# Softmax attention on one core: the later query half's sums from ScalarE in query layout, maxima turned per group, and a list-scheduled order

## The chip, the cores and the metric

The kernel runs on one core of one Trainium2 chip. The metric is device time in microseconds (us). A core has five engines that run in parallel, each through its own instruction stream: TensorE (PE in the profile; its weight loads are PEld), VectorE (DVE), ScalarE (ACT), GpSimd (POOL) and SyncE (SP, which here only issues DMAs). They wait for each other through semaphores. TensorE writes to PSUM, which has 8 banks of 512 fp32 columns on 128 partitions.

## The reference

Six blocks follow one another on x of 2 x 1024 tokens of width 128: a routed feed-forward (8 experts), a gated linear attention, the same feed-forward again, a second routed feed-forward, a softmax attention, and that feed-forward again. The change touches the softmax attention alone:

```python
q = embedded @ Wq.T + bq          # likewise k and v; 16 heads of width 8
qk = jnp.einsum('bhqd,bhkd->bhqk', q, k) / jnp.float32(np.sqrt(s))
p = jax.nn.softmax(qk, axis=-1)
mask = jnp.triu(jnp.ones((s, s), dtype=p.dtype), k=0)
p = p * mask                      # after the softmax, not before it
z = jnp.einsum('bhqk,bhkd->bhqd', p, v)
x = embedded + z                  # then a layer norm with gamma and beta
```

The sequence that is run has 1024 tokens in each of 2 batches. The mask keeps keys k >= q. Since it is applied after the softmax, each query's denominator takes all 1024 keys, while its value sum takes only the keys from the query on. For the later query half (queries 512 to 1023) the keys 0 to 511 enter the denominator and nothing else.

## The kernel before

The 16 heads of the 2 batches form GR = 8 groups of 4 heads. For each group the kernel works over query tiles i (0 to 7, of 128 queries) and key tiles j (0 to 7, of 128 keys). In the plan (`attention_plan`, which returns one list that every engine walks) each item is a letter:

- A: the scores of one head and one query tile against all 1024 keys, in query layout (queries on partitions): two bf16 matmuls of 512 columns (line 770) into one of two slots of two PSUM banks each. VectorE then reduces the 1024 columns to the negative row maximum (line 1342). A slot is free again when the reduction is done (`wait_slot`). There are 256 A tiles.
- S and M: when one head has its four tiles of a query half, GpSimd splits the maxima into three bf16 parts (lines 1444 to 1447, four operations), TensorE turns them (line 778), ScalarE copies them out (line 970), and SyncE stores them as three further rows of that head's queries (line 505). The next score matmul thus subtracts the maximum by itself. There are 64 of these turns.
- B: the scores again, now in key layout (keys on partitions), of one head and one key tile against 512 queries, maximum subtracted: one bf16 matmul of 512 columns (line 795) into a ring of NBB = 3 banks, which the turns M share. ScalarE takes exp of it into SBUF, in a ring of NPT = 12 (line 987). The ring bank is free when that exp is done (`wait_ring`).
- V: for one step (one key tile, four heads) the fp32 matmuls of the probabilities with the values and with a column of ones (line 828) into the one PSUM bank that is left. The four heads stand in four column groups of TensorE and run side by side. A step whose key tile crosses the diagonal has up to three parts: `denominator` (sum alone), `both` (values and sum) and `masked` (values of the 128x128 block after GpSimd's triangle, line 1454). For the later query half the key tiles 0 to 3 are `denominator` alone, 512 columns wide.
- T: after two groups, sixteen transposes of the result (line 783) into the A slots, which VectorE divides out (lines 1356 and 1357). C, part of V in the plan before, is ScalarE's copy of the result bank (line 994).
- Z: pieces of the next layer norm of the first batch, on VectorE, with two changes of ScalarE's function table.

`STEPS` holds per group 8 steps for the earlier query half and 8 for the later one, so 16 steps of four B and one V. The order is written by rule: 20 A tiles come first, then A tiles are spread evenly between the B's (`want`), and they end 8 steps before the last step. Each V stands one step behind its B's. SyncE loads the operands of group G + 3 (lines 481 and 484) when group G is done.

## Time and profile before

| | us |
|---|---|
| median of 3 runs | 973.85 |
| lowest, highest | 973.75, 978.03 |
| the profiled execution, its time | 973.44 |
| its span in the profile | 971.7 |
| attention stage, first score matmul to the end of the last turn | 409.40 to 850.15 |

The page splits the span into 40 slices of about 24.3 us and gives the busy share of each engine in tenths:

```
PE   4042867504214965299999999999899999830794
DVE  5216599631521437596877777768977776062243
ACT  2021500203102643216877676766767777720462
PEclk9995899657555995658999999998999999965697
```

Slices 17 to 35 are the attention. A digit is an average: what decides is which engine the others wait for inside a step, and that is read from the timeline. The clock row is the clock granted to TensorE, 9 or more standing for full speed. Matmul lengths in the profile contain the time through the pipeline, so the cost of a matmul in a stream is read from the distance between starts.

### The profile page before, as it was taken

To read this page: it belongs to the slowest core of one execution; us is meant where nothing else is said; L and a number is where in the kernel's file an instruction comes from. 1 tells how busy PE (TensorE), PEld (TensorE's weight loads), DVE (VectorE), ACT (ScalarE), POOL (GpSimd) and SP (SyncE) were. 2 spreads that over 40 slices of the span, in tenths; PEclk is the share of its full clock that TensorE was granted. 3 is DMA by queue.
4 is the path that set the end of the run, shared out by engine and by line. 5 is a ranking of instruction groups with operands and counts; after the bars stand their busy time and mean duration, and the time that the engine had idled before them with its cause. 6 is when DMAs were issued, how large, how long until landed. Compare 5 with 4: busy or idle time off the path is not lost.

```text
span 971.7 us, 13757 instructions
## 1 busy us (share of the span) xinstructions
PE 671.2 (69%) x4446; PEld 331.9 (34%) x4446; DVE 571.0 (59%) x1035; ACT 443.7 (46%) x836; POOL 299.9 (31%) x679
## 2 busy tenths in 40 slices
PE   4042867504214965299999999999899999830794
PEld 4031322403213962113333333242233433230693
DVE  5216599631521437596877777768977776062243
ACT  2021500203102643216877676766767777720462
POOL 0606156151633440012233223230323233105242
PEclk9995899657555995658999999998999999965697
...
DMA packets 45926, 44.89 MB, mean 46 GB/s; under 512 B 5904, under 2 KB 36316, under 8 KB 45600
## 3 DMA queue, kind: packets, MB, share of 16 engines
q1 hardware_dynamic: 41168, 35.90, 15.8%
...
q10 hardware_dynamic: 144, 0.51, 0.2%
...
## 4 chain that ended last, share of the span: by engine, by line
PE 56%; DVE 16%; issue 8%; POOL 8%; DMA 7%; ACT 4%; SPq 1%; POOLq 0%; ACTq 0%; DVEq 0%
PE PS L828 14%; PE PS L795 12%; PE PS L770 11%; PE PS L628 5%; PE PS L639 4%; POOL slots_x L1389 4%; DVE ARENA L1342 3%; POOL ARENA L1403 2%; DVE ARENA L1312 2%; PE PS L535 2%; ACT ARENA L987 2%; DMA ARENA<-slots_x 2%; DVE XN L1042 2%; DVE PS L1304 1%; POOL ARENA L1414 1%
## 5 line engine op out<-in xcount | busy, mean ns | idle before, releaser
L1342 DVE TENSOR_REDUCE ARENA<-PS 128x1 f32<-128x1024 f32 x256 | 303.0, 1220 | 94.2 <-PE PS L770 93.7
L987 ACT ACTIVATE ARENA<-PS 128x512 f32<-128x512 f32 x512 | 279.6, 597 | 95.8 <-PE PS L795 89.3
L795 PE MATMUL PS<-ARENA 75*128 75x512 bf16 x512 | 175.0, 388 | 8.3 <-ACT ARENA L987 6.8
L770 PE MATMUL PS<-ARENA 72*128 72x512 bf16 x512 | 164.5, 406 | 21.1 <-DMA ARENA<-k_parts 16.6
L828 PE MATMUL PS<-ARENA 128*8 128x128 f32 (+8 forms) x1920 | 153.3, 435 | 0.7 <-ACT ARENA L987 0.7
L1454 POOL TENSOR_SCALAR_AFFINE_SELECT ARENA<-ARENA 128x128 f32<-128x128 f32 x256 | 74.6, 296 | 160.6 <-ACT ARENA L987 160.4
L580 PE MATMUL PS<-C,ARENA 128*128 128x128 f32 x78 | 17.1, 369 | 120.0 <-DMA ARENA<-slots_x 119.9
L1272 DVE TENSOR_TENSOR ARENA<-PS,ARENA 128x512 f32<-128x512 f32 x46 | 31.8, 692 | 96.1 <-PE PS L628 96.1
L553 PE MATMUL PS<-C,XN 128*128 128x128 f32 x96 | 24.5, 407 | 90.9 <-DVE XN L1042 89.9
L795 PEld LDWEIGHTS PS<-ARENA 75*128 75x128 bf16 x512 | 47.5, 98 | 105.6 <-ACT ARENA L987 56.8
L770 PEld LDWEIGHTS PS<-ARENA 72*128 72x128 bf16 x512 | 44.8, 100 | 103.9 <-issue 37.1
L894 ACT COPY ARENA<-PS 128x512 f32<-128x512 f32 (+1 forms) x20 | 11.5, 573 | 134.3 <-PE PS L580 134.3
L828 PEld LDWEIGHTS PS<-ARENA 128*32 128x32 f32 (+2 forms) x1920 | 43.7, 98 | 76.1 <-issue 38.7
L1396 POOL DMA_INDIRECT tokens_y<-ARENA x46 | 44.7, 972 | 74.8 <-DVE ARENA L1281 73.8
L1444 POOL CAST ARENA<-ARENA 128x4 bf16<-128x4 f32 x64 | 12.1, 189 | 174.2 <-DVE ARENA L1342 174.1
L580 PEld LDWEIGHTS PS<-C,ARENA 128*128 128x128 f32 x78 | 12.2, 188 | 123.3 <-issue 119.3
L628 PE MATMUL PS<-ARENA 128*128 128x128 f32 x368 | 53.6, 293 | 1.1 <-ACT ARENA L917 0.7
L639 PE MATMUL PS<-ARENA 128*128 x368 | 51.5, 284 | 1.5 <-ACT ARENA L928 1.5
L1414 POOL TENSOR_TENSOR ARENA<-ARENA 128x1024 f32<-128x1024 f32 x16 | 37.6, 2351 | 46.2 <-DVE ARENA L1312 44.0
L1389 POOL DMA_INDIRECT slots_x<-ARENA,SCATI x32 | 31.4, 983 | 63.7 <-DVE ARENA L1222 55.2
L553 PEld LDWEIGHTS PS<-C,XN 128*128 128x128 f32 x96 | 16.5, 208 | 97.9 <-DVE XN L1042 86.6
L1389 POOL DMA_INDIRECT slots_x<-XN,SCATI x32 | 31.3, 978 | 60.1 <-DVE SCATI L1242 51.0
...
## 6 DMA issues: line engine op xcount, KB each, us to landing
...
```

What stands on the lines that cost most here:

```text
L553: i = nc.tensor.transpose(PS[:, c % 2, (t % 4) * P:(t % 4 + 1) * P], XN[:, t, 0:P], ident)
L628: ins = nc.tensor.matmul(PS[:, 4 + i % 2, f * P:(f + 1) * P], W1[:, i % 2, f * P:(f + 1) * P], XST[:, i * P:(i + 1) * P], start=True, stop ...
L639: ins = nc.tensor.matmul(o, HG[:, i % 2, f * P:(f + 1) * P], WT[:, bass.ds(owner[i] * WB + F1 + f * P, P)], start=(f == 0), stop=(f == FB ...
L770: ins = nc.tensor.matmul(PS[:, slot + c, :], Q3[0:KQ, G % Q3R, g, i * P:(i + 1) * P], K3[0:KQ, G % Q3R, g, c * 512:(c + 1) * 512], start=T ...
L795: nc.tensor.matmul(PS[:, bank, 0:w], K3[0:MR + 3, G % Q3R, i, j * P:(j + 1) * P], Q3[0:MR + 3, G % Q3R, i, half * 512:half * 512 + w], sta ...
L828: ins = nc.tensor.matmul(PS[32 * g:32 * g + width, 7, lo:hi], v, probs, start=(what == "denominator" and st in (0, TB)), stop=(j == TB - 1 ...
L987: nc.scalar.activation(PT[:, n % NPT, 0:w], PS[:, 4 + ring_number[x] % NBB, 0:w], ACT.Exp).then_inc(b_exp, 1)
L1342: nc.vector.tensor_reduce(NM[:, k % 4, i:i + 1], PS[:, slot:slot + 2, :].rearrange("p b n -> p (b n)"), AX.X, ALU.max, negate=True).then_i ...
L1389: pool.indirect_dma_start(sx[k], bass.IndirectOffsetOnAxis(ap=SCATI[:, t:t + 1], axis=0), src[:, t, :], None, bounds_check=slots - 1, oob_ ...
L1396: pool.indirect_dma_start(ty, bass.IndirectOffsetOnAxis(ap=XS[:, i, P:P + 1].bitcast(U32), axis=0), EO[:, i, :], None, bounds_check=N - 1, ...
L1414: nc.gpsimd.tensor_tensor(QS[:, n % 8, :], QT[:, b * S:(b + 1) * S], ST[:, n % 2, :], ALU.mult).then_inc(qs_done, 1)
L1454: nc.gpsimd.affine_select(out=MD[:, n % NPT, :], in_=PT[:, n % NPT, diag:diag + P], compare_op=ALU.is_ge, fill=0.0, base=0, pattern=[[-1, P]],
```

## The change

**Fewer key-layout steps.** The later half's steps over key tiles 0 to 3 are gone: `STEPS` has 12 steps per group (96 in all, 128 before). The remaining four steps of the later half (key tiles 4 to 7) take only the query tiles that their values need, 256, 256, 384 and 512 columns (`columns`), and their `denominator` parts are as narrow.

**The missing sums in query layout.** ScalarE takes exp of the scores with the maximum as its bias and lets the accumulator output add up the row. For query tiles 6 and 7 (`DIRECT`, items X) it reads A's own slot, 768 and 896 columns, after VectorE's reduction; the slot stays taken until then. For tiles 4 and 5 (`AGAIN`, items D) TensorE computes the 512 columns once more into the ring. The exps themselves go to a scratch area (`SPARE`). Per group, four fp32 matmuls against the identity (item N) add these sums into the result bank ahead of the later half's first V. `DEN` and `SPARE` lie over weights of the first feed-forward, which are no longer in use.

**Maxima turned per group.** One S, M and copy now serve four heads (48 rows), 16 in all where there were 64. SyncE issues four row stores behind each, and the first B of a group's half waits for all four.

**The order.** `attention_plan` now simulates the engines with a table of costs (`WEIGHT`) and takes at each moment the item of the lowest rank that can start. It returns a list for each engine. The A tiles are planned to end 12 steps before the last one (`TAIL`), with at least 18 first.

```diff
 HQ = TB // 2
-STEPS = [(0, j) for j in range(TB)] + [(1, j) for j in range(TB)]
+MW = 4 * HQ
+DIRECT = (6, 7)
+AGAIN = (4, 5)
+STEPS = [(0, j) for j in range(TB)] + [(1, j) for j in range(HQ, TB)]
 NS = len(STEPS)
+FIRST = {0: 0, 1: TB}
+LEAD = 2
+TAIL = 12
...
+WEIGHT = {"A": 0.44, "M": 0.3, "D": 0.22, "T": 0.6, "N": 0.9, "max": 1.19, "split": 0.95, "mask": 0.29, "rows": 4.5,
+          "copy": 0.59, "turn": 0.9, "load": 8.0, "Z": 1.2}
+HOP = 0.1
...
+def columns(m):
+    half, j = STEPS[m % NS]
+    if half == 0:
+        return 4 * P, (P * j if j < HQ else None)
+    last = max(i for i in range(HQ, TB) if i <= j or i in AGAIN)
+    return P * (last - HQ + 1), P * (j - HQ)
+def v_parts(m):
+    half, j = STEPS[m % NS]
+    w, diag = columns(m)
+    if diag is None:
+        return [(0, w, "both" if half == 0 else "denominator")]
+    parts = [(diag, w, "denominator")]
+    if diag > 0:
+        parts.append((0, diag, "both"))
+    return parts + [(diag, diag + P, "masked")]
...
+    ahead = 4 * HQ + LEAD
...
+        if last_turns:
+            offer(-1, "T", slot_free(slots, NA), last_turns[0][0])
+        if at < len(tiles):
+            G = tiles[at][1] // 4
+            share = 1.0
+            if b < 4 * steps:
+                m, g = divmod(b, 4)
+                share = min(1.0, (done_by[m] + (done_by[m + 1] - done_by[m]) * g / 4) / done_by[-1 - TAIL])
+            rank = 0 if at < ahead + (len(tiles) - ahead) * share else 5
+            offer(rank, "A", slot_free(slots, NA), 0.0 if G < Q3R else finished.get(G - Q3R))
+        if to_turn:
+            offer(0.5, "M", slot_free(ring, NBB), to_turn[0][0])
+        if again:
+            offer(1.5, "D", slot_free(ring, NBB), again[0][0])
+        if b < 4 * steps and b < 4 * v + NPT:
+            m, g = divmod(b, 4)
+            G, (half, j) = m // NS, STEPS[m % NS]
+            offer(1, "B", slot_free(ring, NBB), rows.get((G, half)) if m % NS == FIRST[half] else 0.0)
+        if 4 * v + 4 <= b:
+            G, (half, j) = v // NS, STEPS[v % NS]
...
+            offer(1.2, "V", *times)
+        return out
...
+        kind = min((x for x in offers if x[0] <= now), key=lambda x: x[1])[2]
+        if kind == "A":
+            _, hh, i = item = tiles[at]
+            at += 1
+            now += WEIGHT["A"]
...
+            if i in DIRECT:
+                held[0] = None
+                later(top + HOP, 0, 0.18 + P * i / 1200, ("X", hh, i), then)
+            elif i in AGAIN:
+                again.append((top + HOP, hh, i))
+            if hh % 4 == 3 and i == tiles_of_unit(h)[-1]:
+                to_turn.append((run("pool", top + HOP, WEIGHT["split"], ("S", G, h)) + HOP, G, h))
+        elif kind == "M":
...
+        DEN = col("f0_w1").rearrange("p (r i c) -> p r i c", r=2, i=HQ)
+        SPARE = C[:, COLS["f0_w2"][0]:COLS["f0_b2"][0] + E * P].rearrange("p (r n) -> p r n", r=2)
...
-                        G, g = divmod(hh, 4)
+                        _, G, h = x
                         tiles = tiles_of_unit(h)
-                        sp.wait_ge(m_copied, maxima_number[hh, h] + 1)
-                        sp.dma_start(Q3[MR:MR + 3, G % Q3R, g, tiles[0] * P:(tiles[-1] + 1) * P],
-                                     MT[0:3 * len(tiles), hh % 4, :]).then_inc(m_rows[hh % 4], 16)
+                        sp.wait_ge(m_copied, maxima_number[G, h] + 1)
+                        for g in range(4):
+                            sp.dma_start(Q3[MR:MR + 3, G % Q3R, g, tiles[0] * P:(tiles[-1] + 1) * P],
+                                         MT[3 * HQ * g:3 * HQ * (g + 1), h, :]).then_inc(m_rows[h], 16)
...
+                    elif i in DIRECT:
+                        pe.wait_ge(x_exp, direct_number[k, i] + 1)
...
+                    elif kind == "D":
+                        G, g = divmod(k, 4)
+                        nc.tensor.matmul(PS[:, bank, :], Q3[0:KQ, G % Q3R, g, i * P:(i + 1) * P],
+                                         K3[0:KQ, G % Q3R, g, 0:512], start=True, stop=True).then_inc(d_scores, 1)
+                    elif kind == "N":
+                        pe.wait_ge(x_exp, 4 * len(DIRECT) * (k + 1))
+                        pe.wait_ge(d_exp, 4 * len(AGAIN) * (k + 1))
+                        pe.wait_ge(z_copied, 2 * k + 1)
+                        for t in range(HQ):
+                            ins = nc.tensor.matmul(PS[:, 7, t * P:(t + 1) * P], DEN[:, k % 2, t, :], ident,
+                                                   start=(t == 0), stop=False, skip_group_check=True)
+                        ins.then_inc(den_added, 1)
                     elif kind == "M":
                         pe.wait_ge(m_split, maxima_number[k, i] + 1)
-                        at, width = unit_columns(i)
-                        o = PS[0:width, bank, 0:P // 2].bitcast(BF16)
-                        nc.tensor.transpose(o, M3[:, k % 4, at:at + width], IDB[:, :]).then_inc(m_turned, 1)
+                        o = PS[0:3 * MW, bank, 0:P // 2].bitcast(BF16)
+                        nc.tensor.transpose(o, M3[:, i, :], IDB[:, :]).then_inc(m_turned, 1)
...
-                            pe.wait_ge(m_rows[i], rows_stored(4 * G + i, half))
+                        if st == FIRST[half]:
+                            pe.wait_ge(m_rows[half], 64 * (G + 1))
...
+                    elif kind in "XD":
+                        G, g = divmod(k, 4)
+                        it = i - HQ
+                        score = score_number["A", k, i]
+                        act.wait_ge(a_max, score + 1)
...
+                        n = lower_number[x]
+                        if n >= 2:
+                            y = lowers[n - 2]
+                            if y[0] == "X":
+                                act.wait_ge(x_exp, direct_number[y[1:]] + 1)
+                            else:
+                                act.wait_ge(d_exp, again_number[y] + 1)
+                        top = NM[:, 1, HQ * g + it:HQ * g + it + 1]
+                        total = DEN[:, G % 2, it, 32 * g + DH:32 * g + DH + 1]
+                        if kind == "X":
+                            slot = 2 * (turn_number["A", k, i] % NA)
+                            w = i * P
+                            scores = PS[:, slot:slot + 2, :].rearrange("p b n -> p (b n)")[:, 0:w]
+                            nc.scalar.activation(SPARE[:, n % 2, 0:w], scores, ACT.Exp, bias=top, accum_out=total
+                                                 ).then_inc(x_exp, 1)
+                        else:
+                            act.wait_ge(d_scores, again_number[x] + 1)
+                            nc.scalar.activation(SPARE[:, n % 2, 0:512], PS[:, 4 + ring_number[x] % NBB, :], ACT.Exp,
+                                                 bias=top, accum_out=total).then_inc(d_exp, 1)
...
+                        if G >= 1 and g == 0 and it == 0:
+                            dve.wait_ge(m_split, maxima_number[G - 1, h] + 1)
+                            if h == 1:
+                                dve.wait_ge(x_exp, 4 * len(DIRECT) * G)
+                                dve.wait_ge(d_exp, 4 * len(AGAIN) * G)
...
+                nc.gpsimd.memset(DEN[:, :, :, :], 0.0).then_inc(den_cleared, 1)
```

TensorE, later query half of the second group (an fp32 matmul is one instruction here and two records in the profile). Before: L795 is B, L828 V, L778 M, L770 A.

```order
L795 MATMUL PS<-ARENA 128x512
L828 MATMUL PS<-ARENA 32x512 x4
L778 MATMUL PS<-IDB,ARENA 12x128
L795 MATMUL PS<-ARENA 128x512 x2
L770 MATMUL PS<-ARENA 128x512 x2
L795 MATMUL PS<-ARENA 128x512
L770 MATMUL PS<-ARENA 128x512 x2
L795 MATMUL PS<-ARENA 128x512
L828 MATMUL PS<-ARENA 32x512 x4
L795 MATMUL PS<-ARENA 128x512 x2
```

After: L918 is A, L925 is D, L933 is N, L978 V, L956 B.

```order
L925 MATMUL PS<-ARENA 128x512 x2
L918 MATMUL PS<-ARENA 128x512 x2
L925 MATMUL PS<-ARENA 128x512 x2
L918 MATMUL PS<-ARENA 128x512 x2
L925 MATMUL PS<-ARENA 128x512 x2
L918 MATMUL PS<-ARENA 128x512 x2
L933 MATMUL PS<-C 128x128 x4
L978 MATMUL PS<-ARENA 32x256 x4
L978 MATMUL PS<-ARENA 8x128 x4
L918 MATMUL PS<-ARENA 128x512 x4
L956 MATMUL PS<-ARENA 128x512 x3
L978 MATMUL PS<-ARENA 32x128 x4
```

The four steps with a `32x512` part alone are gone; D, N and a narrower V stand in their place, and the B's of three steps stand ahead of this piece.

TensorE at the end of that group and the start of the third. Before, an M (L778) stands in every second step:

```order
L828 MATMUL PS<-ARENA 32x256 x4
L828 MATMUL PS<-ARENA 9x256 x4
L828 MATMUL PS<-ARENA 8x128 x4
L795 MATMUL PS<-ARENA 128x512
L778 MATMUL PS<-IDB,ARENA 12x128
L795 MATMUL PS<-ARENA 128x512
L770 MATMUL PS<-ARENA 128x512 x2
L795 MATMUL PS<-ARENA 128x512
L770 MATMUL PS<-ARENA 128x512 x2
```

After, one M (L939) serves four heads; the first B (L956) of the new group stands behind it, with A, D, a V and the turns T (L944) between:

```order
L918 MATMUL PS<-ARENA 128x512 x2
L939 MATMUL PS<-IDB,ARENA 48x128
L978 MATMUL PS<-ARENA 32x128 x4
L978 MATMUL PS<-ARENA 9x384 x4
L978 MATMUL PS<-ARENA 8x128 x4
L918 MATMUL PS<-ARENA 128x512 x2
L925 MATMUL PS<-ARENA 128x512
L918 MATMUL PS<-ARENA 128x512 x2
L925 MATMUL PS<-ARENA 128x512 x2
L944 MATMUL PS<-C,ARENA 128x128 x16
L956 MATMUL PS<-ARENA 128x512 x3
```

The single M has moved ahead of the group's last V, and everything behind the first B waits in TensorE's order if that B's rows are late.

ScalarE, about one group. Before, L987 is the exp of B and L970 the copy of M:

```order
L987 ACTIVATE ARENA<-PS 128x512 x4
L970 COPY MT<-PS 12x128
L987 ACTIVATE ARENA<-PS 128x512 x8
L970 COPY MT<-PS 12x128
L987 ACTIVATE ARENA<-PS 128x512 x8
L970 COPY MT<-PS 12x128
L987 ACTIVATE ARENA<-PS 128x512 x8
```

After, L1135 is the exp of B, L1159 is X, L1163 is D, L1122 and L1170 are the copies of M and C:

```order
L1159 ACTIVATE C<-PS,ARENA 128x896
L1135 ACTIVATE ARENA<-PS 128x512 x3
L1122 COPY MT<-PS 48x128
L1135 ACTIVATE ARENA<-PS 128x512 x5
L1163 ACTIVATE C<-PS,ARENA 128x512 x2
L1170 COPY ARENA<-PS 128x512
L1135 ACTIVATE ARENA<-PS 128x256 x8
L1135 ACTIVATE ARENA<-PS 128x384 x4
L1163 ACTIVATE C<-PS,ARENA 128x512 x6
```

The copies of M are fewer; X of 768 and 896 columns, and D, stand in the same queue as the exps that V waits for.

## Rows read from the trace of the kernel before

**Rows 1.** The page: busy time by engine, and the chain that ended last.
```profile
PE 671.2 (69%) x4446; PEld 331.9 (34%) x4446; DVE 571.0 (59%) x1035; ACT 443.7 (46%) x836; POOL 299.9 (31%) x679
...
PE 56%; DVE 16%; issue 8%; POOL 8%; DMA 7%; ACT 4%; SPq 1%; POOLq 0%; ACTq 0%; DVEq 0%
```

**Rows 2.** Windows, attention stage (columns: busy us and instructions by engine, granted clock, DMA).
```profile
434.00:640.00 206.00, 202.69 (x1532) 71.62 (x1532) 154.41 (x133) 150.48 (x300) 60.91 (x259) 0.98 0.11 20
824.00:851.00 27.00, 22.40 (x186) 7.39 (x185) 1.55 (x4) 18.80 (x36) 4.71 (x16) 1.00 0.00 1
409.00:851.00 442.00, 422.65 (x3072) 143.10 (x3072) 322.78 (x336) 304.93 (x601) 121.50 (x512) 0.95 0.12 22
```

**Rows 3.** Groups of instructions by line (busy us, mean ns, idle before and its releasers).
```profile
L1342 DVE TENSOR_REDUCE ARENA<-PS 128x1 f32<-128x1024 f32 x256 | 303.0, 1220 | 94.2 <-PE PS L770 93.7
L987 ACT ACTIVATE ARENA<-PS 128x512 f32<-128x512 f32 x512 | 279.6, 597 | 95.8 <-PE PS L795 89.3
L795 PE MATMUL PS<-ARENA 75*128 75x512 bf16 x512 | 175.0, 388 | 8.3 <-ACT ARENA L987 6.8 <-ACT MT L970 0.8 <-DMA ARENA<-MT 0.7
...
L970 ACT COPY MT<-PS 12x128 bf16<-12x128 bf16 x64 | 15.8, 246 | 46.3 <-PE PS L778 46.2
```

**Rows 4.** Timeline of one ordinary step (start us, length us, engine, line, instructions).
```profile
562.52 0.59 PE L770 MATMUL PS<-ARENA 72*128 72x512 bf16 x2
...
562.96 0.60 PE L795 MATMUL PS<-ARENA 75*128 75x512 bf16 x2
...
563.48 1.07 PE L828 MATMUL PS<-ARENA 128*32 128x512 f32 x8
...
564.48 0.60 PE L770 MATMUL PS<-ARENA 72*128 72x512 bf16 x2
```

**Rows 5.** Timeline of TensorE, three diagonal steps, the last two with a maxima turn between.
```profile
592.55 1.29 PE L828 MATMUL PS<-ARENA 128*32 128x384 f32 x24
...
595.61 1.29 PE L828 MATMUL PS<-ARENA 128*32 128x256 f32 x24
...
598.34 0.39 PE L795 MATMUL PS<-ARENA 75*128 75x512 bf16 x1 [0.21 <-ACT ARENA L987]
...
599.32 1.29 PE L828 MATMUL PS<-ARENA 128*32 128x128 f32 x24
```

**Rows 6.** Timeline at the start of the stage.
```profile
410.44 26.04 DVE L1342 TENSOR_REDUCE ARENA<-PS 128x1 f32<-128x1024 f32 x22 [10.37 <-PE PS L770]
...
432.96 0.26 ACT L970 COPY MT<-PS 12x128 bf16<-12x128 bf16 x1 [4.45 <-PE PS L778]
...
433.73 0.63 PE L795 MATMUL PS<-ARENA 75*128 75x512 bf16 x1
...
435.01 1.49 PE L795 MATMUL PS<-ARENA 75*128 75x512 bf16 x3
```

**Rows 7.** Row stores by their line (length of an issue, min/median/max ns).
```profile
L505 SPq DMA_DIRECT2D ARENA<-MT x64: 697/698/849, 419.1 to 824.0; - x64
```

**Rows 8.** Timeline, last steps and last turn of the stage.
```profile
828.89 1.07 PE L828 MATMUL PS<-ARENA 128*32 128x512 f32 x8
...
831.29 1.06 PE L828 MATMUL PS<-ARENA 128*32 128x512 f32 x8
...
842.74 2.07 ACT L987 ACTIVATE ARENA<-PS 128x512 f32<-128x512 f32 x4 [0.55 <-PE PS L795]
...
848.10 2.05 PE L783 MATMUL PS<-C,ARENA 128*128 128x128 f32 x16 [0.80 <-ACT ARENA L994]
```

**Rows 9.** Groups by line: a ScalarE operation whose bias is read from SBUF.
```profile
L933 ACT ACTIVATE ARENA<-PS,C 128x512 f32<-128x512 f32 x4 | 2.4, 689 | 0.0
```

**Rows 10.** Windows of 2 us around a fall of the granted clock.
```profile
702.00:704.00 2.00, 0.63 (x4) 0.22 (x4) 1.78 (x4) 1.99 (x4) 0.29 (x1) 1.00 0.69 84
706.00:708.00 2.00, 2.00 (x21) 0.82 (x24) 0.00 (x0) 0.60 (x1) 0.56 (x3) 0.50 0.51 111
```

**Rows 11.** Timeline: one value step at the lower clock.
```profile
671.94 1.94 PE L828 MATMUL PS<-ARENA 128*32 128x512 f32 x8
```

309 lines of the change are left out of this document (184 added, 125 removed).

## The prediction

> **What bounds the kernel now.** I read the page first. It shows TensorE on 56% of the chain that ended last, and no other engine above 16% [rows 1]. Then the windows. In the attention stage TensorE is busy for 422.65 of 442 us, VectorE for 322.78 and ScalarE for 304.93 [rows 2]. The reader is to see that TensorE is the wall there with some 100 us between it and the next engine. The groups say the same from the other side: VectorE's reductions idle 94.2 us, 93.7 of them for the score matmuls of A, ScalarE's exps idle 95.8 us, 89.3 for the matmuls of B, while B itself lost only 8.3 us [rows 3]. So work taken from TensorE is worth its time, until another engine stands in the way. How far away those are decides the size.
>
> **Prices on TensorE**, from distances between starts. An A is 0.44 us (562.52 to 562.96), two B's up to a V 0.52, so a B is 0.22 to 0.26 (I take 0.24), and a V of 512 columns 1.00 [rows 4]. A diagonal step without a turn is 3.06 (592.55 to 595.61). Less two A's and four B's that leaves 1.22 for its V of 640 columns in all. From 512 to 640 columns a V thus grows by 0.22; I price one of 384 at 0.79. The next step, with one turn M in it, is 3.71, so an M costs 0.65, of which 0.21 is a wait for the ring of three banks [rows 5].
>
> **What goes.** Per group four steps of the later half: four V of 1.00 and sixteen B of 0.24, 7.8 us, in 8 groups 62.7. The other four steps of that half have V's of 384, 384, 512 and 640 columns in place of 640 each: 3.80 for 4.88, in all 8.6. Their B's lose 256, 256 and 128 of 512 columns, four heads each. A B's price over 512 columns gives at most 1.2 per group, 9.6 in all; since narrow ones keep their overhead I take 8.5. Of 64 turns 48 go. At 0.65 each that is 31; without the ring wait 0.44, or 21.
>
> **What comes.** 64 D's, each like a B: 15. Eight N's of four fp32 matmuls of 128 columns over the full array: a V part of 512 columns costs 1.00, the sixteen turns at the end 2.05 [rows 8], so between 0.5 and 1.2 each, I take 1.0: 8. Net on TensorE: 62.7 + 8.6 + 8.5 + 31 - 15 - 8 = 88 (77 with the cheap M). If nothing else stood in the way, the stage would end at 762 where it now ends at 850.15.
>
> **What else stands in the way.** VectorE still reduces 256 tiles, 22 of them in 26.04 us, 1.18 each [rows 6]: 303 us, and 19.8 us of other work in the stage (322.78 less 303.0) [rows 2, 3]. Starting at 410.44 it is done with the reductions at about 732 at the earliest. Behind the last A the plan leaves more than a half group, some 24 us. So VectorE alone allows no end before about 756. ScalarE gains nothing: per group its columns are 32,768 as before. A 512-column exp in a stream costs 0.49 (four in 2.07) [rows 8]. The copies of M show 0.25 for 128 columns and the exps 0.60 for 512 [rows 3], 0.9 ns per column. A bias from SBUF adds 0.09 (689 for 597) [rows 3, 9]. An X of 832 columns in the mean is then 0.87, a D 0.58. Per group: 32 x 0.49 + 8 x 0.26 + 4 x 0.37 + 4 x 0.49 for B, 8 x 0.87 for X, 8 x 0.58 for D, 1.7 of copies, about 34.5 us, where 64 x 0.49 + 8 x 0.25 + 1.2 = 34.6 stood before. What the accumulator output adds no row shows. Its lower end is nothing; its upper end is a further short operation, 0.25 [rows 3]. I take 0.1, since it goes with an instruction that is there already.
>
> **The sum goes by stretches**, because the engines bind in turn. The order of the changed kernel has about 16 A's beside a group's earlier half and 16 beside the rest.
> - Start: 16 tiles at 1.18 from 410.44 end at 429.4. GpSimd's split (1.0, four operations as before), turn and copy end near 431.2. Then four row stores of 0.70 each are issued one behind another [rows 7]. One store now lands at most 2.6 us behind the copy: it ended at 433.22, and the fourth head's B, third in the row from 435.01, needed it [rows 6]. With 2.1 us more for the other issues the first B starts at about 436, where now it is 433.73. The wait is filled with A's.
> - Earlier half, 8 steps: TensorE per step 4 x 0.24 + 2 x 0.44 + 1.11 = 2.95; ScalarE 4 x 0.49 + 0.87 = 2.83, VectorE 2.37. TensorE binds, just: 23.6, with one M 24.2.
> - Later half: TensorE 16 A's 7.0, B's 2.8, V's 3.8, D's 1.9, N 1.0, M 0.65, 17.2; VectorE 16 x 1.18 = 18.9. VectorE binds: 18.9.
> - Seven groups at 43.1: 302.
> - Three pairs of turns T at 2.05, 6. The norm pieces (VectorE has 19.8 less 6 for the turns) fall half into stretches where VectorE binds, 8. Function table changes, 3.
> - Last group: four steps with A's, 12.4 with M. Then four steps at 2.40, as the last steps now run [rows 8], 9.6 and an M 0.65; sixteen narrow exps and four D's on ScalarE, 5.5; N, four V's and their gaps, 5.5: 21. Copy and last turn, 2.8.
> Sum: 436 + 302 + 17 + 12.4 + 21 + 2.8 = 791, so 59 less than 850.15. The MEMSET of `DEN` and the changed buffers lie beside the projections. Nothing after the stage changes. The profiled execution took 973.44 us (span 971.7), so 973.44 - 59 = 914; the median 973.85 is 0.4 higher. I forecast 915.
>
> The waits added: TensorE at N waits for eight X, eight D and the copy C, with the later half's V's queued behind; they are cheap and their exps have run ahead. A's second next waits for X, so VectorE can lose 0.4 (X's 0.98, TensorE's 0.44 and two hops, less the other tile's 1.18) up to 0.9 per pair of X tiles, 32 pairs: 13 to 29 where no TensorE wall hides it. In the earlier half it does, and most X stand there: I take 0.
>
> **Rivals.**
> (a) *ScalarE binds the earlier half.* For it: 2.83 against 2.95 is no margin. With 0.25 for the accumulator a step is 3.08, 0.13 more, 8 us over 60 steps, and X's behind exps of B hold A's slots, 13 to 29 us. Against it: the plan gives X the first place. Time 915 + 8 + 17 = 940.
> (b) *The engines interleave without loss*, norm pieces and turns included, and only VectorE's queue and the tail are left: end at 756 to 762, time 883. Against it: now, with one clear bound, ScalarE still lost 0.21 here and 0.44 per step there.
> (c) *Slower: the rows arrive late.* The first B of each group half waits for four stores in place of one, and all A's, D's and V's behind it in TensorE's order stand. Between M and that B there are a V, two A's, three D's and turns, 1.2 + 0.9 + 0.7 + 2.1 = 4.9 us, where there is a pair of turns, else 2.8; copy, issues and landing take 0.26 + 4.7. At 15 starts the gain is gone if each waits 3.9 us; with 5 us each the time is 915 + 75 = 990. Against it: now all B's together lost 0.7 us to stores [rows 3], and a plan made with their latency puts other work in.
> (d) *The clock falls.* The granted clock was 1.00 while TensorE was busy for 0.63 of 2 us, and 0.50, 1.2 of 2.4 GHz, two windows later [rows 10]. There a V took 1.94 in place of 1.07 [rows 4, 11]. The changed stage has work for TensorE for 8 x 41.4 = 331 of its 382 us, so it pauses more. If a third of the 64 earlier-half steps ran at 1.2 GHz (V 1.94, four B's and two A's at twice their price, 5.6 for 2.95), that is 21 x 2.7 = 57, time 971: no change. Against it: in the last steps, with a pause of 0.4 in each 2.4 us, the clock stayed at 1.00 [rows 2, 8].
> The Trainium skill, TensorE: Matmul & The Clock Gate, section "A second HAM failure mode: psum-queue depth-cycling", speaks for (d): a kernel that cycled through PSUM banks with small idle times between groups of matmuls had its clock swing between the two levels, and lost throughput by it. This stage cycles through three banks and two slots in just that way. By that rule (d) would be the forecast, 971. The trace does not bear it out for small regular pauses, only for the large one, so it gets little weight.
>
> **How the numbers follow.** The forecast, TensorE and VectorE in turn: 0.58, with 902 to 930 as its own range. (a) 0.20, (b) 0.08, (c) 0.06, (d) 0.05, something between (a) and (c) 0.03. What a measurement of this kernel can tell from no change is about 0.5%, 5 us. Faster: 0.58 + 0.20 + 0.08 + 0.03 and 0.02 of (d) and 0.01 of (c), 0.92. Same: 0.03 of (d). Slower: 0.05 of (c). The range goes over most of (a) and stops short of (b): 892 to 950.
>
> **What would show it.** Right: no 512-column `denominator` V in the later half; the T pairs 86 to 90 us apart; the granted clock near 1.00; the first B near 436; reductions back to back from each group's last wide V to the next group's first B, with waits for TensorE between; X at 0.9 to 1.1 us. Wrong: X above 1.3 us, A's waiting for ScalarE for more than 15 us in total, B's waiting for row stores for more than 20 us, or windows of the stage at 0.50.

## The result, and the profile after

The changed kernel takes 982.65 us (median of 20 runs, 973.8 to 999.73), the one before 974.65 (20 runs, 973.45 to 978.19). The ratio is 1.0041, 95% interval 1.0024 to 1.0058. Where a median and a ratio part in this section or below, it is because the ratio leaves disturbed runs out; the sums below go by the ratios, in hundredths of about 974 us. The forecast was 915, 892 to 950. The gain did not come, and the time lies outside the range.

The page after, to hold against [rows 1] and the clock row shown with the time before:

```profile
PE 660.2 (67%) x4142; PEld 336.5 (34%) x4142; DVE 569.6 (58%) x1035; ACT 445.2 (45%) x916; POOL 266.5 (27%) x488
...
PEclk9995879657556995656999996996689998765697
...
PE 45%; DVE 21%; issue 11%; DMA 8%; POOL 8%; ACT 6%; SPq 1%; POOLq 0%; ACTq 0%; DVEq 0%
```

TensorE has 304 fewer matmul records and only 11 us less busy time. The clock row has fallen to 6 at slices 19, 25, 28 and 29 of the attention, where it showed 8, 9, 8 and 9 before. Both point to the same place: the matmuls are fewer but longer.

The windows of the stage, as in [rows 2] (busy us and instructions of PE, PEld, DVE, ACT, POOL; granted clock; DMA). First the stretch from the first B to the end of the last turn, of after and then of before:

```profile
440.68:861.61 420.93, 384.33 (x2722) 141.87 (x2720) 295.93 (x314) 301.68 (x671) 86.70 (x316) 0.88 0.09 16
440.00:460.00 20.00, 20.00 (x88) 6.19 (x90) 10.78 (x9) 12.32 (x24) 4.67 (x16) 0.50 0.00 1
680.00:720.00 40.00, 33.30 (x174) 11.82 (x173) 27.58 (x42) 16.40 (x38) 7.50 (x27) 0.59 0.18 31
720.00:800.00 80.00, 72.49 (x545) 26.30 (x541) 66.16 (x78) 63.52 (x142) 17.82 (x65) 1.00 0.01 2
```

```profile
433.73:850.14 416.41, 400.61 (x3027) 139.71 (x3025) 298.73 (x315) 303.49 (x597) 118.41 (x496) 0.98 0.09 16
```

The reader is to see three things. The stretch is not shorter (420.9 for 416.4) though TensorE is busy 16 us less. In 20 us of it TensorE was busy for all 20 at 0.50, 1.2 GHz, doing 88 records, where 80 us at 1.00 did 545. And VectorE and ScalarE have the same busy time as before, so neither got more work.

**An accounting that can be made of any run.** Windows of 1 us give the granted clock. The sum of twice (1 - clock) is the time at 1.2 GHz, *low*; half of it is how much longer TensorE was busy for the same work (at most, since it was not busy in all of it), so *work* = busy - low/2. The length is work + idle + low/2. The forecast's row is the prediction's own sum by stretches: 8 x 41.4 = 331 for all steps, and 8 for the four sets of turns T, less 10 for the 22 A's and two D's that stand ahead of the first B.

| first B to the end of the last turn, us | length | work | idle | low | low/2 |
|---|---|---|---|---|---|
| before | 416.4 | 390.7 | 15.8 | 19.8 | 9.9 |
| forecast (436 to 791) | 355 | 329 | 26 | 0 | 0 |
| after | 420.9 | 331.5 | 36.6 | 105.7 | 52.9 |

TensorE did lose 59 us of work. Lower clock (43 more) and idle time (21 more) took them back. Against the forecast the stretch is 66 us too long: 53 clock, 11 of idle time, 2 of work. The net of 88 us in the prediction was another reckoning, of the difference to before; it was 29 too high, but the forecast time was not made from it. The first B stands at 440.68 for 436; of this 3.8 us is the first A (413.21 for 409.40), ahead of the change's work.

The groups by line, to [rows 3] and [rows 9]:

```profile
L1523 DVE TENSOR_REDUCE ARENA<-PS 128x1 f32<-128x1024 f32 x256 | 301.1, 1219 | 103.7 <-PE PS L918 102.6
L1159 ACT ACTIVATE C<-PS,ARENA 128x896 f32<-128x896 f32 x32 | 32.7, 1021 | 0.2
L1159 ACT ACTIVATE C<-PS,ARENA 128x768 f32<-128x768 f32 x32 | 28.8, 901 | 4.3 <-DVE ARENA L1523 4.3
L1163 ACT ACTIVATE C<-PS,ARENA 128x512 f32<-128x512 f32 x64 | 43.5, 701 | 2.9 <-PE PS L925 2.6
L1163 ACT ACTIVATION_READ_ACCUMULATOR C<-PS,ARENA 128x1 f32 x64 | 14.0, 219 | 0.0
L1159 ACT ACTIVATION_READ_ACCUMULATOR C<-PS,ARENA 128x1 f32 x64 | 13.5, 211 | 0.0
L956 PE MATMUL PS<-ARENA 75*128 75x512 bf16 (+2 forms) x384 | 122.5, 396 | 9.7 <-ACT ARENA L1135 5.9 <-DMA ARENA<-MT 2.9
L933 PE MATMUL PS<-C 128*128 128x128 f32 x64 | 12.7, 361 | 5.9 <-issue 5.8
L1122 ACT COPY MT<-PS 48x128 bf16<-48x128 bf16 x16 | 4.2, 260 | 54.1 <-PE PS L939 53.8
```

X lasts what I had taken (0.90 and 1.02, for 0.9 to 1.1), and D 0.70. The accumulator output is an instruction of its own, 0.21 to 0.22 us, 27.5 us in all by the lengths. It overlaps the exp before it, though: from one start to the next it adds 0.09 (under e_noacc), where I had 0.1. B's waited only 2.9 us for row stores, but N (L933), whose waits I had put at nothing, had 5.9 us of idle time before it. VectorE's reductions are as little the wall as before.

The timeline of TensorE, with SyncE's stores and ScalarE's X, at a fall of the clock (start, length, engine, line; idle before and its releaser in brackets):

```profile
586.74 0.22 PE L939 MATMUL PS<-IDB,ARENA 128*48 128x128 bf16 x1 [0.34 <-POOL ARENA L1628]
...
587.28 2.92 SPq L649 DMA_DIRECT2D ARENA<-MT  x4
587.42 1.29 PE L978 MATMUL PS<-ARENA 128*32 128x128 f32 x24
...
589.26 0.91 ACT L1159 ACTIVATE C<-PS,ARENA 128x768 f32<-128x768 f32 x1
590.06 0.20 ACT L1159 ACTIVATION_READ_ACCUMULATOR C<-PS,ARENA 128x1 f32 x1
...
590.31 0.60 PE L918 MATMUL PS<-ARENA 72*128 72x512 bf16 x2 [0.63 <-ACT C L1159]
...
591.39 0.38 PE L956 MATMUL PS<-ARENA 75*128 75x512 bf16 x1 [0.48 <-DMA ARENA<-MT]
...
602.81 2.36 PE L978 MATMUL PS<-ARENA 128*32 128x384 f32 x24
```

And windows of 1 us over it, in the columns of the windows above:

```profile
590.00:591.00 1.00, 0.60 (x2) 0.11 (x2) 0.56 (x2) 1.00 (x5) 0.00 (x0) 1.00 0.03 6
591.00:592.00 1.00, 0.40 (x2) 0.13 (x3) 1.00 (x1) 1.00 (x3) 0.00 (x0) 1.00 0.34 94
592.00:593.00 1.00, 1.00 (x5) 0.47 (x6) 0.57 (x2) 1.00 (x3) 0.00 (x0) 1.00 0.75 201
593.00:594.00 1.00, 0.76 (x5) 0.20 (x3) 1.00 (x2) 0.81 (x3) 0.36 (x2) 0.76 0.69 107
600.00:601.00 1.00, 1.00 (x4) 0.33 (x3) 0.73 (x1) 1.00 (x2) 0.29 (x1) 0.50 0.55 98
```

At the start of a group's first half A waits for X (0.63), B for the rows (0.48), and the next A again for X (0.20): 1.3 us of pause within 3 us. Then the clock is at 0.50 from 594 to 610 with TensorE busy throughout, and a step whose 24 records took 1.29 takes 2.36. There are nine such stretches after, of 3 to 24 us, the first from 440 to 460; before had three, 20 us in all. By the Trainium skill, TensorE: Matmul & The Clock Gate, section "A second HAM failure mode: psum-queue depth-cycling", small idle times between groups of matmuls let the clock swing; the trace of after agrees, where that of before had not shown it.

The largest single wait of after stands at another turn, where the stores (L649) go out at once but land behind the operand loads (L625, L628) in SyncE's queue:

```profile
701.83 0.97 SPq L628 DMA_DIRECT2D ARENA<-k_parts  x3
702.51 0.83 PE L918 MATMUL PS<-ARENA 72*128 72x512 bf16 x2 [0.53 <-DVE ARENA L1523]
...
703.73 0.27 PE L939 MATMUL PS<-IDB,ARENA 128*48 128x128 bf16 x1 [0.38 <-POOL ARENA L1628]
...
704.32 2.98 SPq L649 DMA_DIRECT2D ARENA<-MT  x4
...
708.50 2.02 PE L918 MATMUL PS<-ARENA 72*128 72x512 bf16 x4 [1.83 <-ACT C L1159]
712.98 1.01 PE L956 MATMUL PS<-ARENA 75*128 75x512 bf16 x2 [2.45 <-DMA ARENA<-MT]
```

The clock fell before that wait. From 699 to 703 TensorE has only A's to issue, one every 1.13 us, and waits 0.26, 0.53, 0.53 and 0.53 us for the reductions; from 703 to 720 it is at 0.50. The changed plan has 11 A's there between the last B of one group and the first of the next, where the plan of before has at most two.

### The profile page after: what moved, and what is told of

Its sections match the earlier page's. It is cut to its first block, busy times and chain, and to the rows that moved or that the text cites. A ratio compares the mean times of both kernels' runs of the same rounds, so it can differ in the third digit from the quotient of the medians.

```text
span 983.1 us, 12946 instructions
## 1 busy us (share of the span) xinstructions
PE 660.2 (67%) x4142; PEld 336.5 (34%) x4142; DVE 569.6 (58%) x1035; ACT 445.2 (45%) x916; POOL 266.5 (27%) x488
## 4 chain that ended last, share of the span: by engine, by line
PE 45%; DVE 21%; issue 11%; DMA 8%; POOL 8%; ACT 6%; SPq 1%; POOLq 0%; ACTq 0%; DVEq 0%
PE PS L978 9%; PE PS L918 9%; DVE ARENA L1523 9%; PE PS L956 7%; PE PS L772 5%; PE PS L783 4%; POOL slots_x L1570 4%; POOL ARENA L1584 2%; DVE ARENA L1488 2%; PE PS L679 2%; DMA ARENA<-slots_x 2%; ACT ARENA L1135 2%; DVE XN L1218 1%; DVE PS L1480 1%; PE PS L933 1%
## 5 line engine op out<-in xcount | busy, mean ns | idle before, releaser
L1523 DVE TENSOR_REDUCE ARENA<-PS 128x1 f32<-128x1024 f32 x256 | 301.1, 1219 | 103.7 <-PE PS L918 102.6
L1135 ACT ACTIVATE ARENA<-PS 128x512 f32<-128x512 f32 (+2 forms) x384 | 188.0, 561 | 79.5 <-PE PS L956 78.1
L918 PE MATMUL PS<-ARENA 72*128 72x512 bf16 x512 | 171.3, 431 | 33.1 <-DMA ARENA<-k_parts 16.6
L956 PE MATMUL PS<-ARENA 75*128 75x512 bf16 (+2 forms) x384 | 122.5, 396 | 9.7 <-ACT ARENA L1135 5.9
L978 PE MATMUL PS<-ARENA 128*8 128x128 f32 (+8 forms) x1664 | 120.0, 417 | 1.8 <-ACT ARENA L1135 1.8
L1448 DVE TENSOR_TENSOR ARENA<-PS,ARENA 128x512 f32<-128x512 f32 x46 | 31.8, 692 | 94.8 <-PE PS L772 94.8
L918 PEld LDWEIGHTS PS<-ARENA 72*128 72x128 bf16 x512 | 39.1, 103 | 127.4 <-DVE ARENA L1523 53.7
L956 PEld LDWEIGHTS PS<-ARENA 75*128 75x128 bf16 x384 | 39.1, 104 | 82.5 <-ACT ARENA L1135 39.5
L978 PEld LDWEIGHTS PS<-ARENA 128*9 128x9 f32 (+2 forms) x1664 | 41.2, 103 | 65.5 <-issue 41.9
L1159 ACT ACTIVATE C<-PS,ARENA 128x768 f32<-128x768 f32 x64 | 61.4, 961 | 4.5 <-DVE ARENA L1523 4.3
L822 PE MATMUL PS<-XNT,C 128*128 128x512 f32 x64 | 36.8, 712 | 17.6 <-DVE ARENA L1488 17.5
```

The source lines that it names most:

```text
L918: ins = nc.tensor.matmul(PS[:, slot + c, :], Q3[0:KQ, G % Q3R, g, i * P:(i + 1) * P], K3[0:KQ, G % Q3R, g, c * 512:(c + 1) * 512], start=T ...
L956: nc.tensor.matmul(PS[:, bank, 0:w], K3[0:MR + 3, G % Q3R, i, j * P:(j + 1) * P], Q3[0:MR + 3, G % Q3R, i, half * 512:half * 512 + w], sta ...
L978: ins = nc.tensor.matmul(PS[32 * g:32 * g + width, 7, lo:hi], v, probs, start=(what == "denominator" and st == 0), stop=(j == TB - 1), ski ...
L1135: nc.scalar.activation(PT[:, n % NPT, 0:w], PS[:, 4 + ring_number[x] % NBB, 0:w], ACT.Exp).then_inc(b_exp, 1)
L1159: nc.scalar.activation(SPARE[:, n % 2, 0:w], scores, ACT.Exp, bias=top, accum_out=total).then_inc(x_exp, 1)
L1523: nc.vector.tensor_reduce(NM[:, h, HQ * g + it:HQ * g + it + 1], PS[:, slot:slot + 2, :].rearrange("p b n -> p (b n)"), AX.X, ALU.max, neg ...
```

## The experiments

Each kernel was timed in five rounds beside the kernel before. After the result my theory was that the small pauses of a stage whose three engines are nearly even bring the clock down. The rivals (the queue theory of some expectations is the last of them) were that TensorE's work was mis-sized, that the turns per group or the new order cost the time by themselves, and that ScalarE sets the pace through X, D and the slots of A that X holds. The accounting for all of them is in a table behind the last one.

**The order and the turns alone (e_order).** The changed order and the turns per group, all sums as before.

```diff
-DIRECT = (6, 7)
-AGAIN = (4, 5)
-STEPS = [...] + [(1, j) for j in range(HQ, TB)]
+DIRECT = ()
+AGAIN = ()
+STEPS = [...] + [(1, j) for j in range(TB)]
-TAIL = 12
+TAIL = 8
```

> The changed kernel without its moved sums: the later half has its 8 steps of 512 columns again, no X, D or N; the maxima turned per group and the list-scheduled order stay. TensorE work is that of before less 48 turns (about 31 us). Clock theory (TensorE that pauses gets the lower clock, and that ate the gain): TensorE stays dense here, under 60 us of low clock in the stage, time 945 to 955. Rival (the list-scheduled order is itself at fault, by late rows and a static order that fits badly): 965 to 985.

Measured: 1029.48, ratio 1.0581 (1.0556 to 1.0606), far above both ranges. Order and turns lose 57 us by themselves, so the moved sums gain 53 in their company. B's waited 12.5 us for row stores here, and low clock was 116 us.

**Without the moved sums (e_nosums).** The changed kernel without X, D and N, whose sums are left out.

```diff
-DIRECT = (6, 7)
-AGAIN = (4, 5)
+DIRECT = ()
+AGAIN = ()
...
-                order["pe"].append(("N", G, 0))
```

> The changed kernel without X, D and N, so the later half's sums over keys 0 to 511 are left out; widths and steps are as in the changed kernel, the order is planned anew. TensorE has still less to do. Queue theory (ScalarE's X and D with their accumulator reads, and the slots that X holds, set the pace): 900 to 920. Clock theory alone: TensorE pauses at least as much, waits for VectorE, low clock above 120 us in the stage, time 940 to 965.

Measured: 942.24, ratio 0.9661 (0.9622 to 0.97). X, D and N cost 37 us. TensorE's part in them is 25 (331.5 less 306.1), where I had 23. But even without them the stretch has 89 us of low clock. The time is that of the clock theory, not of the queue theory (900 to 920).

**More work for TensorE (e_busy).** The first matmul of the tiles 0 to 3 of every head is issued twice, 128 more.

```diff
-                        for c in range(2):
+                        for c in ((0, 0, 1) if i < HQ else (0, 1)):
```

> The changed kernel with the first score matmul of every A of query tiles 0 to 3 issued twice, into the same bank: 128 matmuls of 0.22 us more, mostly beside the later half, where VectorE was to bind. Clock theory: fewer falls of the clock, low clock from 137 to under 90 us, time 10 to 25 us less than the changed kernel. Queue theory: added work on TensorE can only cost, time 0 to 20 us more.

Measured: 988.62, ratio 1.017 (1.0139 to 1.0201), 13 us over the changed kernel for 21 us of added work. This is the rival's range; the clock theory had 10 to 25 us less. Low clock did go down, from 106 to 76 us in the profiles. From the mean granted clock of each run the whole program has 383 us of it on average, 402 in the changed kernel: half of these 19 is near the 8 us between.

**Less work for TensorE in the kernel before (e_less_pv).** Three of the later half's four wide sums over 32 columns only (their rest left out).

```diff
-                            parts.append((0, w, "both" if half == 0 else "denominator"))
+                            parts.append((0, 32 if half and j else w, "both" if half == 0 else "denominator"))
```

> The kernel before, with the sums of three of the four later-half steps over keys 0 to 511 taken over 32 of 512 columns (the sums are left out there): 24 V of 1.00 us become about 0.2, order and all else unchanged, so 19 us of TensorE work less. If TensorE's work alone sets the pace: 955. If the clock takes it back when TensorE thins out: low clock rises from 50 us by 20 or more and the time is 962 to 974.

Measured: 965.13, ratio 0.992 (0.9887 to 0.9953), 8 us less. In its profile the work fell by 16.5 and the length by 9.9; idle time rose by 2.5 and low clock by 8.3 (20 or more expected), half of which, 4.1, counts. Here, with an order made for the old balance, the work taken away is already worth only 50 to 60%.

**Turns per group, in the order by rule (e_rule).** The kernel before, with one S and M per group half. Its plan already put the first B of a half behind the turn of the half's fourth head; now it stands behind the one turn, and four A's further back.

```diff
-LEAD = 0
+LEAD = 4
...
-    ahead = turns.index(("M", 3, 0)) + 1 + LEAD
+    ahead = turns.index(("M", 0, 0)) + 1 + LEAD
...
-                want = max(want, turns.index(("M", 4 * G + 3, s // TB)) + 1 + LEAD)
+                want = max(want, turns.index(("M", G, s // TB)) + 1 + LEAD)
```

> The kernel before with one change alone: maxima turned once per group (16 turns, four row stores each), in the order written by rule, the first B of a group half at least 4 A's behind its turn. All sums as before. If the turn per group is cheap and the list-scheduled order lost the time (1029 us with it): 940 to 960. If the turn per group itself costs, through A's that must bunch ahead of a group and rows that arrive late: 975 to 1010.

Measured: 1025.52, ratio 1.0514 (1.0477 to 1.0551), 50 us slower, more than either range had, with the part that I had down for a gain of 31. TensorE's work fell by only 6 (384.7). Its timeline, around one group half's end (L796 is A, L834 B, L856 V, L822 T):

```profile
642.69 1.03 PE L796 MATMUL PS<-ARENA 72*128 72x512 bf16 x4
644.61 0.60 PE L796 MATMUL PS<-ARENA 72*128 72x512 bf16 x2 [0.89 <-DVE ARENA L1398]
645.74 0.60 PE L796 MATMUL PS<-ARENA 72*128 72x512 bf16 x2 [0.53 <-DVE ARENA L1398]
646.18 0.85 PE L834 MATMUL PS<-ARENA 75*128 75x512 bf16 x3
646.96 2.36 PE L856 MATMUL PS<-ARENA 128*32 128x128 f32 x24
```

All A's of a half, and eight more (four in before), must be issued before its first B, and those that are late are issued in a row: in the later groups this plan has 3 to 6 A's between two B's there, where before had at most two. TensorE waits for the reductions (an A every 1.13 us here; 20.0 us in all, 3.5 in before), and the clock falls behind it: V of 24 records 2.36 us. Both kernels need the maxima of all four heads there, so the run does not say how much of the 50 us belongs to the one turn with its four stores (B's waited 4.4 us for them) and how much to the four A's more.

**A larger lead (e_lead8, e_order8).** `LEAD` 2 becomes 8 in the changed kernel and in e_order. In e_order's plan the A's between the last B of a half and the first of the next go from 3 to 8 down to 0 to 5 (none at the last half in either). The changed kernel's plan hardly moves: the A's issued by each half's first B differ by two at most, and the row of 11 stays.

> The changed kernel with LEAD 8 in place of 2 in its planner: A's run six tiles further ahead, so that a group's rows are stored before its first B's turn comes. If late rows and the A's bunched ahead of each group make the pauses in which the clock falls: pauses fewer, low clock under 100 us in the stage, time 945 to 965. If X and D at the group's start make them: within 8 us of the changed kernel's 982.

> The kernel with list-scheduled order and turns per group but all sums as before (1029 us), with LEAD 8 in place of 2. It waited 17 us for row stores and VectorE waited 149 us for A. Late rows as the cause: 970 to 990. The greedy order itself (A's with low rank wait behind B's until the share asks for them): 1010 to 1030.

Measured: e_order8 990.0, ratio 1.0157 (1.0131 to 1.0183), 41 us less than e_order, at the edge of what late rows had (970 to 990). e_lead8 976.97, ratio 1.0004 (0.9968 to 1.004): 4 less than the changed kernel, and the intervals overlap. With the old sums the bunching is thus what the turns per group cost. For the changed kernel e_lead8 does not test it, since its plan is nearly the same.

**Without the accumulator output (e_noacc).** X and D keep their exps; the sums are left out.

```diff
-nc.scalar.activation(SPARE[:, n % 2, 0:w], scores, ACT.Exp, bias=top, accum_out=total
+nc.scalar.activation(SPARE[:, n % 2, 0:w], scores, ACT.Exp, bias=top
```

> The changed kernel without accumulator outputs: X and D compute their exps but no sum is kept (the later half's sums over keys 0 to 511 are left out); 128 accumulator reads of 0.21 us go, order and all else unchanged. Queue theory: ScalarE's 27 us less, TensorE's waits for X and D shrink, time 955 to 970. If ScalarE's length is not what paces the stage: 975 to 985.

Measured: 966.63, ratio 0.9891 (0.9858 to 0.9924), 15 us less, as the queue theory had it. Six D's stand in a row; here are the first two of them in the changed kernel, then all six in this one:

```profile
630.70 0.69 ACT L1163 ACTIVATE C<-PS,ARENA 128x512 f32<-128x512 f32 x1
631.27 0.21 ACT L1163 ACTIVATION_READ_ACCUMULATOR C<-PS,ARENA 128x1 f32 x1
631.36 0.70 ACT L1163 ACTIVATE C<-PS,ARENA 128x512 f32<-128x512 f32 x1
```

```profile
616.67 3.58 ACT L1163 ACTIVATE C<-PS,ARENA 128x512 f32<-128x512 f32 x6
```

From start to start a D takes 0.66 us there and 0.57 here; X's differ by 0.09 too. The 128 outputs thus held ScalarE for 12 us, not for the 27.5 of their lengths, and the kernel got back about all of it. So ScalarE's time seems to count in full here, though it is busy for only 302 of 421 us; in the profiles it came back as 4.8 us less idle time of TensorE and 15 less low clock.

**Turns per head, with the changed sums and order (e_head), and list order alone (e_order_head).** One S, M and store per head, as before, in the changed kernel and in e_order.

```diff
-            if hh % 4 == 3 and i == tiles_of_unit(h)[-1]:
-                to_turn.append((run(..., ("S", G, h)) + HOP, G, h))
+            if i == tiles_of_unit(h)[-1]:
+                to_turn.append((run(..., ("S", hh, h)) + HOP, hh, h))
```

> The changed kernel with the maxima turned per head again (64 turns, one row store each, the first B of a head waits for its own store only); moved sums and list-scheduled order stay, planned anew with the shorter store. If the turn per group makes the pauses (A's bunched ahead of a group, rows late by four stores): TensorE and clock recover, time 940 to 960. If X and D make them: 975 to 990, since 48 turns of TensorE come back.

> List-scheduled order alone: turns per head, all sums as before (16 steps per group). With turns per group this took 1029 us. If the turn per group is the fault and the list-scheduled order is neutral: 968 to 982. If the order itself is at fault: above 1000.

Measured: e_head 998.58, ratio 1.0173 (1.0125 to 1.0222); e_order_head 993.12, ratio 1.019 (1.0163 to 1.0218). So the list order alone costs 18 us. The profile of e_order_head is of a slower run (1000.6); half of the 20.7 us of idle time in it is one wait, a row store behind a group's loads:

```profile
711.92 0.74 SPq L650 DMA_DIRECT2D ARENA<-MT  x1
721.00 1.44 PE L958 MATMUL PS<-ARENA 75*128 75x512 bf16 x3 [9.55 <-DMA ARENA<-MT]
```

The turns also get their true price here: work 391.4 with 64 turns and 375.4 with 16, 16 us for 48, 0.33 each. And e_head against e_order_head shows that the moved sums gain next to nothing with turns per head: 43 us of work less, 6 us more idle, 75 us more low clock. Against the changed kernel e_head is 13 us slower: beside the moved sums the turns per group save time, and undoing them was no remedy (expected 940 to 960). e_head with `LEAD` 6 was no better (1004.11).

**Pauses put into the kernel before (e_drain).** At each group half TensorE waits until all exps and reductions so far are done. Nothing else changes.

```diff
+                            if i == 0 and k > 0:
+                                pe.wait_ge(b_exp, 4 * k)
+                                pe.wait_ge(a_max, sum(y[0] == "A" for y in plan[:at]))
```

> The kernel before with a pause: at each group half (15 times) TensorE waits until ScalarE has done all exps and VectorE all reductions given to it so far. Direct cost at most 2 us each, 15 to 30 in all. If a short pause lowers the clock and that costs more than itself: low clock rises from 20 us to above 60 after the first B, and the time to 1010 or more. If pauses cost only themselves: 985 to 1003.

Measured: 1005.81, ratio 1.0324 (1.0296 to 1.0352). In the profile the work is nearly the same (389.5), with 17.8 us more idle time and 30.6 us more low clock: 17.8 + 15.3 - 1.2 = 31.9, by which the stretch is longer. The pauses put in cost 1.8 times the idle time that they add, and the surplus is the clock. The time lies between the two expectations, and the low clock (50 us) stayed under the 60 of the first. Not every pause brings it: four of 1.0 to 1.3 us, between 569 and 649, brought no low clock.

**Loads behind the stores (e_late), and with the larger lead (e_lead8_late).** SyncE issues a group's loads after the next turn's row stores.

```diff
-                            sp.wait_ge(pv_done, NS * (G + 1))
-                            load_group(G + Q3R)
+                            held.append(G)
+                    if x[0] == "M" and held:
+                        G = held.pop()
+                        sp.wait_ge(pv_done, NS * (G + 1))
+                        load_group(G + Q3R)
```

> The changed kernel with SyncE's loads of a group's operands issued behind the next turn's row stores, not ahead of them. In the changed kernel one turn found the load of a group ahead of it and the first B came 9 us after it, with 17 us of low clock around it. If that queue matters: time 965 to 975. If it is an incident: within 4 us of the changed kernel's 982.

Measured: 981.34, ratio 1.0069 (1.0043 to 1.0095), and 979.06, ratio 0.9988 (0.9946 to 1.003). For the changed kernel the queue of loads is an incident, not the cause.

**The order by rule with the moved sums (e_even).** Turns per head, A evenly spread, X one tile and D two behind their A.

> Moved sums, turns per head, and in place of the list schedule an order by rule: A's spread between the B's in proportion to the work of the steps, each X one tile and each D two tiles behind its A. TensorE's work as in the kernel with turns per head and list schedule (998 us). If the list-scheduled order makes the pauses and through them the low clock: low clock under 60 us after the first B and 925 to 955. If X and D with their accumulator reads pace the stage whatever the order: 975 to 1000.

Measured: 1087.19, ratio 1.1123 (1.1073 to 1.1172). The group of its A (L1057 is X):

```profile
L815 PE MATMUL PS<-ARENA 72*128 72x512 bf16 x512 | 198.6, 482 | 79.4 <-ACT C L1057 49.7
```

Far above both ranges. Here the slot that X holds counts: TensorE stood 49.7 us before A for X. But it is not all. Against before the stretch is 119 us longer: work 62 less, idle time 60 more, low clock 242 more, 121 by half.

**The slot not held (e_noslot).** X reads constants from SBUF in place of the scores (its sums are thus not those wanted).

```diff
-                    elif i in DIRECT:
-                        pe.wait_ge(x_exp, direct_number[k, i] + 1)
...
-                            slot = 2 * (turn_number["A", k, i] % NA)
-                            scores = PS[:, slot:slot + 2, :].rearrange("p b n -> p (b n)")[:, 0:w]
+                            scores = col("a0_wv", 0, w)
```

> The changed kernel with X reading as many columns of constant weights in SBUF in place of the score slot (the later half's sums are not those of the scores there), so that A's slot is free after VectorE's reduction; ScalarE's instructions, their lengths and the order stay. If the held slots make the pauses: TensorE's wait for X (8.4 us) and VectorE's behind it go, falls of the clock at group starts with them, time 950 to 965. If ScalarE's length or the turn per group is what counts: 975 to 985.

Measured: 980.66, ratio 1.0000 (0.9965 to 1.0035), 4 us less than the changed kernel, with intervals that overlap. With the larger lead and late loads as well (e_noslot8) the median was 973.66, six runs from 958.37 to 975.99; 940 to 955 was expected if the effects add. In the list order the slot costs little, as I had taken it.

**More added work, no sums (e_nosums_busy).** e_nosums with the first matmul of every A issued twice.

```diff
-                        for c in range(2):
+                        for c in (0, 0, 1):
```

> The changed kernel without the three moved operations (X, D and N, their sums left out, as in e_nosums: 942.2 us, low clock 88 us in its profile after the first B), and with the first matmul of every tile of A issued twice, so that TensorE has 256 matmuls of 0.22 us more, 56 us, at full clock. Clock theory (the low clock comes from TensorE having too little to do between its pauses): the low clock falls from 88 to under 40 us, which gives back some 24 to 30 us of the 56, and some more lies in idle time that is there already (30 us): 942 + 56 - 28 - 15 = 955, at most 965. Rival (the added work is only a cost, the clock falls by the pauses whatever TensorE has between them): 985 to 1000, with a low clock near 88.

Measured: 974.38, ratio 0.999 (0.9968 to 1.0011), 32 over e_nosums, between the two. The profiles have 49 us more work, 10 less idle and 18 less low clock, 9 by half: 30. The clock theory in the form in which I gave it falls (71 us, not under 40). Work between pauses helps a little; it does not hold the clock up.

| first B to the end of the last turn, us | length | work | idle | low | ratio |
|---|---|---|---|---|---|
| before | 416.4 | 390.7 | 15.8 | 19.8 | 1 |
| e_less_pv | 406.5 | 374.2 | 18.3 | 28.1 | 0.992 |
| e_drain | 448.3 | 389.5 | 33.6 | 50.4 | 1.0324 |
| e_even | 535.5 | 329.0 | 75.8 | 261.4 | 1.1123 |
| e_order_head | 444.1 | 391.4 | 20.7 | 64.0 | 1.019 |
| e_rule | 454.6 | 384.7 | 34.3 | 71.3 | 1.0514 |
| e_order | 470.4 | 375.4 | 36.8 | 116.4 | 1.0581 |
| e_order8 | 432.1 | 377.9 | 20.7 | 67.2 | 1.0157 |
| after | 420.9 | 331.5 | 36.6 | 105.7 | 1.0041 |
| e_lead8 | 404.5 | 335.6 | 37.2 | 63.3 | 1.0004 |
| e_late | 423.8 | 332.1 | 33.5 | 116.4 | 1.0069 |
| e_noslot | 414.3 | 332.2 | 35.2 | 94.0 | 1.0000 |
| e_noacc | 408.0 | 330.9 | 31.8 | 90.6 | 0.9891 |
| e_busy | 423.4 | 352.3 | 33.0 | 76.2 | 1.017 |
| e_head | 444.6 | 348.3 | 26.6 | 139.3 | 1.0173 |
| e_nosums | 379.1 | 306.1 | 28.6 | 88.8 | 0.9661 |
| e_nosums_busy | 408.7 | 355.1 | 18.2 | 70.9 | 0.999 |

These columns are of one profiled execution each. Where the low clock lies changes from run to run, so lengths part by up to some 10 us from what the ratios say; e_lead8 was profiled at 968.01, with a median of 976.97. Of the 106 us of the changed kernel 20 stand at the first B, where e_lead8, e_late and e_noacc have 7 to 8.

What a microsecond of low clock costs can be read from the changed kernel's 20 runs, where nothing else was altered. Twice (1 - mean granted clock) times the span gives 382 to 439 us of low clock in the whole program. The time rises by 0.41 us per us of it, and by 0.35 over the 14 fastest runs. An estimate by these slopes: the 106 us in the stage cost 37 to 43 us rather than 53, and 86 more than before cost 30 to 35. The pauses that come with a lower clock are within the slopes, so they are high if anything.

## Why the prediction was wrong

By parts, with the ratios: list order +18 (0 in the forecast), turns per group +38 on top, moved sums -53 on top. The sum is +4. In another sequence: list order +18, moved sums -2, turns per group -13. So the turns cost 38 us beside the old sums and save 13 beside the moved ones, and the parts have no prices of their own. In TensorE's work the prediction had -31 for the turns and -57 for the sums, net of D and N.

The view of the bound was right as far as it went: TensorE was the wall [rows 1 to 3]. What work taken from it was worth hung on the rest: 8 us for 16.5 (e_less_pv), 2 for 43 (e_head against e_order_head), 53 for 44 (the changed kernel against e_order).

- **The sum by stretches, 436 + 302 + ... = 791,** is the step that failed. It let the engines bind in turn at full clock, with 26 us of idle time for TensorE. TensorE's work in it was right, 329 for 331.5 (in part by luck: its 16 turns M at 0.65 are 5 us too much, and the rest is 8 too cheap). The measured stretch has 36.6 us of idle time and 52.9 of longer matmuls. VectorE bound no half: its reductions still wait 102.6 us for A, though the later half should have shown them back to back. Pairs of turns T came 104, 119 and 95 us apart where 86 to 90 were forecast, and 103, 114 and 95 before.
- **The clock at 1.00** is the largest term that was missed in it, 53 us in the stage by the accounting, 37 to 43 by the slopes, where I had none; it was rival (d), given 0.05. Its size (57) and its time (971) were near; the place was not, since the stretches lie at the group halves and run on for 3 to 24 us. I let one row decide, a regular pause of 0.4 in 2.4 us in the tail, and did not ask what pauses the new order would have where three engines are nearly even. e_drain shows in the old kernel that pauses of 1 to 3 us can bring it.
- **"Of 64 turns 48 go. At 0.65 each that is 31"** was mis-sized: TensorE's work in them is 0.33 each (16 us), half of it; the rest of [rows 5] was wait. The term stands in the net of 88, not in the 791. What no term had is that one turn for four heads changes when the A's must be issued (e_order against e_order_head +38, and -41 with e_order8's lead).
- **The V's, B's and their prices (62.7 + 8.6 + 8.5 = 80)**: work of e_order less e_nosums, 69. **D and N (23)**: 25, right. With the turns that is 16 + 69 - 25 = 60, and 59 measured, where the net said 88.
- **The accumulator at 0.1** holds, 0.09 from start to start. But the step's 2.83 for ScalarE left it out; with it the step is 2.93, beside TensorE's 2.95. By e_noacc it is worth 15 us. That ScalarE had no margin is what rival (a) said, with 0.25 for it and 25 us in all; it was a part, not the explanation.
- **The slot at 0** holds within 4 us (e_noslot). **N's waits**, called cheap, were 5.9 us. **Rival (c)**: stores cost B's 2.9 us; the exposure is real once a group's load stands before them, 2.45 here and 9.55 in e_order_head. In e_order B's waited 12.5 us for stores. **The start** is 1 us later than forecast, beside the 3.8. Of my four signs of being wrong only the windows at 0.50 showed: X took 0.9 to 1.02 us, and A's waited 7.4 us for X.

What is left open: what decides how long the clock stays low. Over the table it goes neither with idle time (18.2 us of it with 71, 37.2 with 63) nor with TensorE's share of work alone, and one program's runs differ in it. No run could hold the clock up; the slopes say what it costs, not that the stage would end so much sooner without it, for none of its runs had less than 382 us of it in the program. Open too is whether the row of 11 A's and its like make the pauses of the changed kernel, since no run took them away. And the 18 us of the list order are explained only in part, by the wait of 9.55 in the one profile.
